# Cross and masked attention: the first scores issued right behind the first values, the squares turned back one step later

## The chip, the cores and the metric

The program runs on one core of a Trainium2 chip. The metric is the device time of one execution in microseconds (us); lower is better. A core has five engines that run their own instruction lists in order and meet at semaphores: TensorE (PE, with its weight loads shown apart as PEld), VectorE (DVE), ScalarE (ACT), GpSimd (POOL) and SyncE (SP), which issues the transfers.

## What is computed

The reference is a chain of four layers, each a cross attention and a feed-forward block, on x of 32 sequences x 128 tokens x 128 features, with a context of 32 x 128 x 96. The change touches the attentions of the first and of the third layer:

```python
x = x + _L0_xattn_ref(_layernorm(x), ctx_768, wq, bq, wk, bk, wv, bv, wo, bo)      # "cross"
...
x = x + _L2_xattn_ref(_layernorm(x), ctx_768, mask_BxS_bk0, Wq, Wkv)                # "masked"

def _L0_xattn_ref(x, y, wq, bq, wk, bk, wv, bv, wo, bo):     # 16 heads of 8 features
    q = x @ wq.T + bq;  k = y @ wk.T + bk;  v = y @ wv.T + bv
    ...
    score = jnp.einsum('bhqd,bhkd->bhqk', q, k) * scale
    attn = jax.nn.softmax(score, axis=-1)
    out = jnp.einsum('bhqk,bhkd->bhqd', attn, v)
    return out @ wo.T + bo
```

The masked one is the same without biases and without the output projection; rows that the mask leaves out get equal weights. Behind the first layer's attention stands a mixture of 8 experts, whose routing (a second layer norm, logits, the choice and the scatter of rows) rides along in the attention's loop.

## The kernel before, in words

The program is a row of phases. Each engine runs all of phase 1, then all of phase 2, and so on. `attention16` (line 310 on) builds three of them: "cross" (starts near 17 us and ends near 300 us of the profiled span), "masked" (near 787 to 1059 us) and "self". Only the first two use the branch that the change touches. "cross" carries the routing of the next block with it (`post` in the code), "masked" carries none.

The work is one sequence (an item, 128 x 128) at a time, 32 items, as a software pipeline written out by hand. `unrolled` yields one step after the other; in step t, `item(lag)` is item t - lag. So one step works on several items, each at another stage, and the order of the calls inside a step is the order in which an engine issues them. For these two phases F = 1, L = 2 and O = L + 4 = 6. One item passes through these stages:

- lag 0 and 1: `stats`, `aggregate` (DVE), `rsqrt` (POOL), `norm` (DVE, L288) give the layer norm h; `pe_hT` (PE, L404) turns h; `a_hT` (ACT, L941) copies it out; `pe_qkv` (PE, L415 and L416) multiplies with the weights of queries, keys and values; `v_qkv` (DVE: L602 and L615 in cross, L605, L607 and L618 in masked) evicts them.
- lag 2 (L): `pe_turn` (L424) turns q and k; `v_kx` (DVE, L708) expands the keys into kx, four masked copies; `a_qT` (ACT, L917) copies the turned queries, after kx. `pe_scores` (PE, L463) computes scores in two halves of 8 heads into the same two PSUM banks, only so that `v_max` (DVE, L716) can take each row's largest. The second half waits until the first maximum is read. `high` (DVE, L704) and `g_low` (POOL, L826) split q and k into exact parts.
- lag 3 (L + 1): `pe_stack_k` and `pe_stack_q` (PE, L430, eight matmuls) turn these parts. `pe_stack_q` waits for the second maximum. `a_qS` (ACT, L931, four copies) and `a_kS` (ACT, L923) copy them out.
- lag 4: `pe_scoresT` (PE, L478) computes the scores with keys on the partitions, in two halves, and `a_exp` (ACT, L954) takes the exponential of each.
- lag 5 (L + 3): `pe_values` (PE, L494) multiplies the first pair and the second pair of head columns with the values. `v_heads` (DVE, L724 and L726) turns the result in 32 x 32 squares and takes the reciprocal of the sums. `normed` (POOL, L736) divides. `v_heads_back` (DVE, L744) turns the squares back into oT.
- lag 6 (O): `pe_out` (PE, L519 in cross, L521 in masked) multiplies oT with the output weights, or only turns it; `v_residual` (DVE, L750) adds it to X.

In cross, `pe_post_route` (L2126, L2134 to L2140) and `pe_post_turn` (L2119) put the routing's matmuls into PE's step, and `v_post_rows` (L2216, L2235, L2223, and in some steps three or four small ones) and `v_route` put its vector work into DVE's.

Each engine's step is one straight list, for PE:

```python
for item in unrolled(last):
    if it := item(L):
        pe_turn(e, it)
    if it := item(L + 1):
        pe_stack_k(e, it)
        pe_stack_q(e, it)
    ...
    if it := item(F):
        pe_qkv(e, it)
    if it := item(O):
        pe_out(e, it)
    if it := item(L):
        pe_scores(e, it, 1)
```

For ACT the step is a_qT, a_qS, a_hT, (routing), a_kS, a_exp half 0, a_exp half 1, and for POOL rsqrt, the output bias (cross), g_low, normed, (routing).

Of the kernel before, what the change touches and what calls it, by code (L numbers as in the profile page):

```python
# [72 lines left out]
def build(nc, a, out):  # L73
    ctx = ExitStack()
    with ctx:
# [233 lines left out]
        def attention16(p, before, kind, post=None):  # L309
# [214 lines left out]
            def tensor(e):  # L524
                before(e)
                e.wait_ge(s_pad, at(s_pad, n_pad))
                e.wait_ge(sem(p + "weights"), 16 * n_loads[p[:2]])
                e.wait_ge(consts_ready, N_CONSTS)
                if post:
                    e.wait_ge(bf_ready, N_BF)  # L530
                if causal:
                    for item in unrolled(last):
                        if it := item(L + 2):
                            pe_scoresT(e, it, 0)
                        if it := item(L):
                            pe_turn(e, it)
                        if post:
                            pe_post_route(e, item)
                        if it := item(L + 3):
                            pe_values(e, it, 0)  # L540
# [4 lines that stand above are left out]
                            pe_scores(e, it, 0)  # L545
                        if it := item(L + 3):
                            pe_values(e, it, 1)
                        if post:
                            pe_post_turn(e, item)
                        if it := item(F):  # L550
                            pe_hT(e, it)
                        if it := item(L):
                            pe_scores(e, it, 1)
                        if it := item(G):
                            pe_gate(e, it)
                        if it := item(L + 2):
                            pe_scoresT(e, it, 1)
# [4 lines that stand above are left out]
                else:  # L562
# [6 lines that stand above are left out]
                        if post:  # L569
                            pe_post_route(e, item)  # L570
                        if it := item(L + 3):
                            pe_values(e, it, 0)
                        if post:
                            pe_post_turn(e, item)
                        if it := item(F):
                            pe_hT(e, it)
                        if it := item(L + 2):
                            pe_scoresT(e, it, 0)
                        if it := item(L):
                            pe_scores(e, it, 0)  # L580
                        if it := item(L + 3):
                            pe_values(e, it, 1)
                        if it := item(F):
# [5 lines that stand above are left out]
                        if it := item(L + 2):  # L589
                            pe_scoresT(e, it, 1)  # L590
# [166 lines left out]
            def vector(e):  # L757
# [5 lines left out]
                if causal:  # L763
                    e.tensor_scalar(w[p + "wo"][:, :], w[p + "wo"][:, :], 0.5, None, ALU.mult).then_inc(s_wo, 1)
                    for item in unrolled(last):
                        if it := item(0):
                            stats(e, it)
                        if it := item(F):
                            v_h2(e, it)
                        if post:  # L770
                            v_post_rows(e, item)
                        if it := item(L):
                            v_max(e, it, 0)
                        if it := item(1):
                            v_y(e, it)
                        if it := item(0):
                            aggregate(e, it)
                        if it := item(F + 1):
                            v_qk_norm(e, it)
                        if it := item(L + 3):  # L780
                            v_heads(e, it)
                            v_heads_back(e, it)
                        if post:
                            post["v_route"](e, item, O)
                        if it := item(L):
                            v_max(e, it, 1)
                        if it := item(F):
                            v_rotate(e, it)
                        if it := item(O):
                            v_residual_self(e, it)  # L790
                        if it := item(G):
                            v_gate(e, it)
                else:
                    for item in unrolled(last):
                        if it := item(L):
                            v_kx(e, it)
                        if it := item(0):
                            stats(e, it)
                        if it := item(F + 1):
                            high(e, it)  # L800
                        if it := item(1):
                            norm(e, it, h[:, it.s, :])
                        if post:
                            v_post_rows(e, item)
                        if it := item(L):
                            v_max(e, it, 0)
                        if it := item(0):
                            aggregate(e, it)
                        if it := item(L + 3):
                            v_heads(e, it)  # L810
                        if post:
                            post["v_route"](e, item, O)
                        if it := item(F):
                            v_qkv(e, it)
                        if it := item(O):
                            v_residual(e, it)
                        if it := item(L):
                            v_max(e, it, 1)
                        if it := item(L + 3):
                            v_heads_back(e, it)  # L820


            def g_low(e, it):
# [1962 lines left out]
```

## Time and profile before

| what | value |
|---|---|
| median of 3 runs | 1929.82 us (1918.54 to 1933.78) |
| the profiled execution, its own time | 1932.14 us |
| its span, first to last instruction | 1930.3 us |
| PE busy | 1573.1 us, 81% |
| DVE busy | 1325.4 us, 69% |
| ACT busy | 958.3 us, 50% |
| POOL busy | 858.7 us, 44% |
| mean granted TensorE clock | 0.879 of full speed |

Busy shares are means over phases with different limits. The granted clock is how much of TensorE's full clock of 2.4 GHz the chip gave; 0.50 is its lower level, 1.2 GHz. A matmul's duration is modelled at its end, so a PE that is shown busy is not PE at its peak. "Idle before" in a row is how long the engine had been idle when the instruction started, with what ended the wait; where it says "issue", the profile shows nothing that the engine waited for.

### The profile page before, as it was taken

To read this page: it belongs to the slowest core of one execution; us is meant where nothing else is said; L and a number is where in the kernel's file an instruction comes from. 1 tells how busy PE (TensorE), PEld (TensorE's weight loads), DVE (VectorE), ACT (ScalarE), POOL (GpSimd) and SP (SyncE) were. 2 spreads that over 40 slices of the span, in tenths; PEclk is the share of its full clock that TensorE was granted. 3 is DMA by queue.
4 is the path that set the end of the run, shared out by engine and by line. 5 is a ranking of instruction groups with operands and counts; after the bars stand their busy time and mean duration, and the time that the engine had idled before them with its cause. 6 is when DMAs were issued, how large, how long until landed. Compare 5 with 4: busy or idle time off the path is not lost. (4 is left out here: it accounts for less than half of the span.)

```text
span 1930.3 us, 37548 instructions
## 1 busy us (share of the span) xinstructions
PE 1573.1 (81%) x11614; PEld 1204.3 (62%) x11614; DVE 1325.4 (69%) x4215; ACT 958.3 (50%) x1953; POOL 858.7 (44%) x1432
## 2 busy tenths in 40 slices
PE   5889985977798989798897788888849699999840
PEld 3556664965677778565554455555539598888730
DVE  4886773348787777567764688888647488888522
ACT  2775562533333334357764577777725344444310
POOL 2444544356300000123322778788654555566426
PEclk9995786978899999669976699999969899999965
DMA  6674203821000000000000000000028100000043
GB/s 195 225 245 168 102 11 133 252 69 41 17 1 2 0 1 1 5 7 8 9 5 1 1 1 1 2 8 8 8 83 263 41 15 13 19 20 19 10 147 87
DMA packets 60786, 108.35 MB, mean 56 GB/s; under 512 B 11715, under 2 KB 49620, under 8 KB 59796
## 3 DMA queue, kind: packets, MB, share of 16 engines
q1 hardware_dynamic: 54452, 93.45, 15.3%
q0 software_dynamic: 6144, 12.60, 2.1%
q8 instruction: 92, 1.51, 0.3%
q14 instruction: 98, 0.80, 0.1%
HBM read 89.49 MB, written 52.17 MB: 73 GB/s over the span
## 5 line engine op out<-in xcount | busy, mean ns | idle before, releaser
L716 DVE TENSOR_REDUCE parts<-PS 128x8 fp32r<-128x1024 f32 x192 | 234.5, 1221 | 135.2 <-PE PS L463 134.8
L954 ACT ACTIVATE P<-PS 128x1024 f32<-128x1024 f32 x192 | 198.3, 1033 | 114.1 <-PE PS L478 114.1
L931 ACT CAST qS<-PS 32x512 fp32r<-32x512 f32 x384 | 220.7, 575 | 17.7 <-PE PS L430 14.3
L279 POOL TENSOR_TENSOR ve<-mv,eps_t 128x1 f32<-128x1 f32 x160 | 31.7, 198 | 349.7 <-DVE mv L275 349.4
L1788 DVE SCALAR_TENSOR_TENSOR X<-PS,wt,X 128x128 f32 (+1 forms) x480 | 134.4, 344 | 49.6 <-PE PS L1631 40.9
L478 PE MATMUL PS<-qS,kS 128*128 128x512 f32 x384 | 163.5, 484 | 0.8 <-ACT P L954 0.7
L1920 ACT ACTIVATE P<-PS,w_f_b 128x512 f32<-128x512 f32 x128 | 88.0, 687 | 142.7 <-PE PS L1612 141.2
L430 PE MATMUL PS<-ident_r,parts 128*128 128x128 f32 x768 | 134.1, 317 | 26.5 <-issue 12.9
L1631 PEld LDWEIGHTS PS<-w_f_w,P 128*128 128x128 f32 x1024 | 130.3, 193 | 39.8 <-issue 27.8
L1631 PE MATMUL PS<-w_f_w,P 128*128 128x128 f32 x1024 | 142.2, 283 | 13.7 <-DVE X L1788 11.8
L430 PEld LDWEIGHTS PS<-ident_r,parts 128*128 128x128 f32 x768 | 116.8, 226 | 47.9 <-POOL parts L826 26.1
L494 PE MATMUL PS<-P,vx 128*32 128x128 f32 x3072 | 142.1, 311 | 5.1 <-ACT P L954 5.0
L845 POOL TENSOR_TENSOR rrs<-rsq,neg_half 128x20 f32<-128x20 f32 x32 | 114.9, 3592 | 48.0 <-DVE rsq L646 47.4
L463 PE MATMUL PS<-kx,qT 32*128 32x512 f32 x384 | 110.4, 571 | 0.0
L494 PEld LDWEIGHTS PS<-P,vx 128*32 128x32 f32 x3072 | 82.5, 121 | 40.5 <-issue 28.3
L281 POOL TENSOR_TENSOR rstd<-ve,neg_half 128x1 f32<-128x1 f32 x160 | 89.9, 562 | 12.5
L826 POOL TENSOR_TENSOR parts<-qk,parts 128x128 fp32r<-128x128 f32 x192 | 84.6, 460 | 7.3 <-DVE parts L704 6.0
L478 PEld LDWEIGHTS PS<-qS,kS 128*128 128x128 f32 x384 | 72.5, 219 | 23.7 <-ACT P L954 11.7
L463 PEld LDWEIGHTS PS<-kx,qT 32*128 32x128 f32 x384 | 40.3, 207 | 71.5 <-issue 61.0
L1444 POOL TENSOR_TENSOR parts<-ident,mx 128x1024 fp32r<-128x1024 f32 x32 | 60.8, 1899 | 53.2 <-DVE mx L1383 53.2
L1843 POOL TENSOR_TENSOR ve<-mv,eps_t 128x4 f32<-128x4 f32 x8 | 1.6, 199 | 180.5 <-DVE mv L1699 180.5
L1319 PE MATMUL PS<-P 128*128 128x128 f32 x512 | 70.1, 280 | 6.5 <-DVE lgD L2263 2.9
(302 smaller groups left out, 4371.6 us busy)
## 6 DMA issues: line engine op xcount, KB each, us to landing
P<-in_f_blob SPq DMA_DIRECT2D x12, 578.0 KB, 4.1
Y<-in_f_blob SPq DMA_DIRECT2D x11, 578.0 KB, 4.4
ctxT<-in_ctxT SPq DMA_DIRECT2D x128, 48.0 KB, 1.7
tok<-hs SPq DMA_DIRECT2D x46, 128.0 KB, 3.4
hs<-yo SPq DMA_DIRECT2D x46, 128.0 KB, 4.1
P<-in_f_blob SPq DMA_DIRECT2D x12, 450.0 KB, 4.6
Y<-in_f_blob SPq DMA_DIRECT2D x11, 450.0 KB, 4.6
w_f_w<-in_f_w SPq DMA_DIRECT2D x2, 1024.0 KB, 5.7
```

The source lines that it names most:

```text
L281: q.tensor_tensor(rstd[:, it.s, :], ve[:, it.s, :], neg_half[:, 0:1], ALU.pow).then_inc(s_rs, 1)
L430: m = e.matmul(TP[which][:, g * T:(g + 1) * T], parts[:, it.s, which, 4 * g:4 * g + 4, :, :].rearrange("p h c d -> p (h c d)"), ident_r[:, ...
L463: m = e.matmul(S_ps[:, i, :], qT[r:r + 32, it.s, :], kx[r:r + 32, it.s % 2, :, :].rearrange("p j t -> p (j t)"), start=not causal, stop=True)
L478: m = e.matmul(ST_ps[:, i, :], kS[:, it.s % 2, g, :], qS[:, it.s % 2, g, :, :].rearrange("p j t -> p (j t)"), start=not causal, stop=True)
L494: m = e.matmul(OB[32 * g:32 * g + 32, pair * T:(pair + 1) * T], vx[:, it.s, 128 * j + 32 * g:128 * j + 32 * g + 32], P[:, it.s % 2, 4 * g ...
L716: e.tensor_reduce(parts[:, it.s, 0, 8 * half:8 * half + 8, 3, 0], S_ps[:, :, :].rearrange("p i (j t) -> p (i j) t", t=T), AXX, ALU.max)\
L845: e.tensor_tensor(rrs[:, :], rsq[:, :], neg_half[:, 0:n_heads], ALU.pow).then_inc(s_rs3, 1)
L931: m = e.copy(qS[r, it.s % 2, :, j, :], TP[0][r, :].rearrange("p (g t) -> p g t", g=4))
L954: e.activation(P[:, it.s % 2, 8 * half:8 * half + 8, :].rearrange("p h t -> p (h t)"), ST_ps[:, :, :].rearrange("p j n -> p (j n)"), ACT.E ...
L1631: m = e.matmul(YP[(n_steps * b + x) % 2][:, s * T:(s + 1) * T], lhs, w2[:, x, t * D:(t + 1) * D], start=(t == 0), stop=(t == tiles - 1))
L1788: m = e.scalar_tensor_tensor(out=X_s, in0=rows, scalar=wt[:, b, s, x:x + 1], in1=X_s, op0=ALU.mult, op1=ALU.add)
L1920: e.activation(gt[:, (x % 2) * tiles + t, :], ZP[i % 4][:, :], ACT.Gelu if kind == "gelu" else ACT.Relu, bias=b1[:, x, t:t + 1]).then_inc( ...
```

## The change

Two calls move, each within its engine's step, in the branch of cross and masked attention. No instruction is added, removed or altered.

```diff
@@ tensor(e), the step of PE
                         if it := item(L + 3):
                             pe_values(e, it, 0)
+                        if it := item(L):
+                            pe_scores(e, it, 0)
                         if post:
                             pe_post_turn(e, item)
                         if it := item(F):
                             pe_hT(e, it)
                         if it := item(L + 2):
                             pe_scoresT(e, it, 0)
-                        if it := item(L):
-                            pe_scores(e, it, 0)
                         if it := item(L + 3):
                             pe_values(e, it, 1)
@@ vector(e), the step of DVE
                         if it := item(F + 1):
                             high(e, it)
+                        if it := item(O):
+                            v_heads_back(e, it)
                         if it := item(1):
                             norm(e, it, h[:, it.s, :])
...
                         if it := item(L):
                             v_max(e, it, 1)
-                        if it := item(L + 3):
-                            v_heads_back(e, it)
```

On PE, in the cross phase behind the stacks of one step, the rows were (L494 the values, L2119 the routing's turn, L404 the turn of h, L478 the scores with keys on the partitions, L463 the scores for the maximum):

```order
L494 MATMUL PS<-P,vx 32x128 [waits values_turned,v,exp]
L494 MATMUL PS<-P,vx 32x128 x7
L2119 MATMUL PS<-ident,hD 128x128 [waits hT,qT,d_h,kx,v]
L404 MATMUL PS<-ident,h 128x128 [waits qT,kx,h]
L478 MATMUL PS<-qS,kS 128x512 [waits exp,qS,kS]
L478 MATMUL PS<-qS,kS 128x512
L463 MATMUL PS<-kx,qT 128x512 [waits mx,kx,qT]
L463 MATMUL PS<-kx,qT 128x512
L494 MATMUL PS<-P,vx 32x128 x8
```

and now are:

```order
L494 MATMUL PS<-P,vx 32x128 [waits values_turned,v,exp]
L494 MATMUL PS<-P,vx 32x128 x7
L463 MATMUL PS<-kx,qT 128x512 [waits mx,kx,qT]
L463 MATMUL PS<-kx,qT 128x512
L2119 MATMUL PS<-ident,hD 128x128 [waits hT,qT,d_h,kx,v]
L404 MATMUL PS<-ident,h 128x128 [waits qT,kx,h]
L478 MATMUL PS<-qS,kS 128x512 [waits exp,qS,kS]
L478 MATMUL PS<-qS,kS 128x512
L494 MATMUL PS<-P,vx 32x128 x8
```

The two L463 rows moved ahead of four others, with the same waits. In masked the L2119 row is absent and the rest is the same.

On DVE, in the cross phase from one step's second maximum to the next step's first, the rows were (L744 turns the squares back, L708 expands the keys, L288 writes h):

```order
L716 TENSOR_REDUCE parts<-PS 128x8 [waits s]
L744 STREAM_TRANSPOSE oT<-oN 128x128 [waits values_normed,out]
L708 TENSOR_TENSOR kx<-PS,jmask 128x512 [waits turn]
L268 BN_STATS bn<-X 128x6 [waits h]
L704 CAST parts<-qk 128x32x24 [waits qkf,tq]
L288 TENSOR_SCALAR h<-X,mv,rstd 128x128 [waits rstd,bn,hps]
L2216 BN_STATS bnD<-X 128x6 [waits done]
L2235 TENSOR_SCALAR hD<-X,mvD,rsD 128x128 [waits d_rstd]
L2223 BN_AGGR mvD<-bnD 128x2 [waits d_bn]
L716 TENSOR_REDUCE parts<-PS 128x8 [waits s,tq]
```

and now are:

```order
L716 TENSOR_REDUCE parts<-PS 128x8 [waits s]
L708 TENSOR_TENSOR kx<-PS,jmask 128x512 [waits turn]
L268 BN_STATS bn<-X 128x6 [waits h]
L704 CAST parts<-qk 128x32x24 [waits qkf,tq]
L744 STREAM_TRANSPOSE oT<-oN 128x128 [waits values_normed,out]
L288 TENSOR_SCALAR h<-X,mv,rstd 128x128 [waits rstd,bn,hps]
L2216 BN_STATS bnD<-X 128x6 [waits done]
L2235 TENSOR_SCALAR hD<-X,mvD,rsD 128x128 [waits d_rstd]
L2223 BN_AGGR mvD<-bnD 128x2 [waits d_bn]
L716 TENSOR_REDUCE parts<-PS 128x8 [waits s,tq]
```

L744 moved behind L708, L268 and L704; between the second maximum and the keys' expansion nothing is left. The lists of ACT, POOL and SP are as before.

## Rows read from the trace of the kernel before

**Rows 1.** The page: granted TensorE clock in 40 slices of 48.3 us.
```profile
PEclk9995786978899999669976699999969899999965
```

**Rows 2.** DVE's L708 by stretch: us, DVE busy (x instructions), PEclk, DMA share, GB/s.
```profile
43.05:145.52 102.47, 9.18 (x14) 1.00 0.71 240
145.52:195.65 50.13, 3.42 (x5) 0.56 0.45 155
195.65:210.50 14.85, 1.30 (x2) 1.00 0.62 222
210.50:250.26 39.76, 2.73 (x4) 0.57 0.12 41
250.26:271.99 21.73, 1.96 (x4) 1.00 0.03 11
...
859.77:985.38 125.61, 11.74 (x19) 1.00 0.03 8
985.38:1031.78 46.40, 3.46 (x5) 0.56 0.01 2
```

**Rows 3.** All engines, masked: us, PE, PEld, DVE, ACT, POOL busy, PEclk, DMA.
```profile
813.53:852.12 38.59, 38.59 (x225) 24.93 (x225) 23.01 (x56) 21.04 (x37) 8.34 (x24) 0.50 0.02 6
859.77:985.38 125.61, 110.71 (x1009) 66.49 (x1010) 99.78 (x254) 93.07 (x162) 37.54 (x108) 1.00 0.03 8
```

**Rows 4.** Waits of DVE, masked, 859.77 to 985.38 us: us in total, times, longest.
```profile
DVE parts L716 <- PE PS L463: 25.2, 18, 1.4
```

**Rows 5.** Waits of DVE, cross, 43.05 to 145.52 us.
```profile
DVE parts L716 <- PE PS L463: 11.7, 14, 2.0
DVE oT L744 <- POOL oN L736: 3.8, 14, 0.5
```

**Rows 6.** Timeline of one masked step: start, us, instructions, [idle before <-releaser].
```profile
922.33 0.30 DVE L744 STREAM_TRANSPOSE oT<-oN 128x128 f32<-128x128 f32 x1
...
922.52 0.63 PE L430 MATMUL PS<-ident_r,parts 128*128 128x128 f32 x4 [0.21 <-issue]
922.56 0.65 DVE L708 TENSOR_TENSOR kx<-PS,jmask 128x512 fp32r<-128x512 f32 x1
...
923.08 0.64 PE L494 MATMUL PS<-P,vx 128*32 128x128 f32 x16
...
923.24 0.27 ACT L917 CAST qT<-PS 128x128 fp32r<-128x128 f32 x1 [0.86 <-DVE kx L708]
...
923.41 2.34 ACT L931 CAST qS<-PS 32x512 fp32r<-32x512 f32 x4
923.78 0.34 DVE L288 TENSOR_SCALAR h<-X,mv,rstd 128x128 f32<-128x128 f32 x1
...
924.91 0.50 PE L463 MATMUL PS<-kx,qT 32*128 32x512 f32 x2
...
925.53 1.23 DVE L716 TENSOR_REDUCE parts<-PS 128x8 fp32r<-128x1024 f32 x1 [1.40 <-PE PS L463]
...
926.41 0.60 PE L416 MATMUL PS<-w_a_wkv,ctxT 96*128 96x256 f32 x2
...
927.38 0.29 DVE L605 TENSOR_SCALAR qk<-PS,keep 128x128 f32<-128x128 f32 x1
```

**Rows 7.** Timeline of one cross step, same columns; PE's first.
```profile
108.15 1.11 PE L430 MATMUL PS<-ident_r,parts 128*128 128x128 f32 x8 [0.32 <-POOL parts L826]
...
112.96 0.60 PE L416 MATMUL PS<-w_a_wkv,ctxT 96*128 96x256 f32 x2
```

**Rows 8.** The same cross step on DVE.
```profile
108.70 0.31 DVE L744 STREAM_TRANSPOSE oT<-oN 128x128 f32<-128x128 f32 x1 [0.26 <-POOL oN L736]
108.94 0.65 DVE L708 TENSOR_TENSOR kx<-PS,jmask 128x512 fp32r<-128x512 f32 x1
...
113.80 0.41 DVE L602 TENSOR_TENSOR qk<-PS,w_a_bqk 128x256 f32<-128x256 f32 x1
```

**Rows 9.** The same cross step on ACT.
```profile
109.79 2.34 ACT L931 CAST qS<-PS 32x512 fp32r<-32x512 f32 x4
```

## The prediction

> **What bounds the two phases.** I read the granted clock over the span first, then stretches of the two phases, then the waits of DVE, then one step of each in order of time. The clock matters because the two phases are where it moves [rows 1]: of the slices of 48.3 us, the fourth to the sixth (cross) show 5, 7 and 8 tenths, the 17th and 18th and the 21st and 22nd (masked) 6, 6, 7 and 6, while the long phases behind (24 to 29, 31 on) stay at 9 and 8. Counted by the keys' expansion L708, one per step, the phases fall into stretches at either level [rows 2]: cross runs 14 + 2 + 3 = 19 steps at the full 2.4 GHz (the stretch to 271.99 counts the step that begins at its edge), at 102.47 / 14 = 7.32 us each in the long one, and 5 + 4 steps mostly at 1.2 GHz, 50.13 / 5 = 10.03 and 39.76 / 4 = 9.94 us each. Masked runs 18 at the full clock (19 with the edge), 125.61 / 18 = 6.98 us each, and 5 at 46.40 / 5 = 9.28; further ones at 1.2 GHz stand at its start.
>
> At 1.2 GHz, PE is the bound: it is shown busy for 38.59 of 38.59 us [rows 3]. At 2.4 GHz it is busy for 110.71 of 125.61 us, 88%, and something else sets the step. In masked DVE has one wait in its step, 25.2 / 18 = 1.40 us before the first maximum L716 [rows 4]; all else that it does is back to back. In cross it has two, 11.7 / 14 = 0.84 before the same L716 and 3.8 / 14 = 0.27 before L744, which waits for POOL's quotients: 1.11 together [rows 5]. So the loop at full clock is DVE's work, plus the detour over PE to the first scores. One masked step shows the detour [rows 6]: L288 writes h until 924.12, PE then turns h and does one half of the other scores, L463 runs from 924.91 to 925.41, and L716 starts at 925.53, 0.12 behind. Yet L463 needs nothing of h. Its inputs are kx (done 923.21) and qT (done 923.51), and PE's first values end at 923.72.
>
> **The change part by part, masked.** L463 moves behind those values: it can run from 923.72 to 924.22, and L716 starts at 924.34 instead of 925.53, 1.19 earlier. DVE gets there in time: L744 takes a slot of 922.56 - 922.33 = 0.23 us, and moving it from ahead of L708 to ahead of L288 leaves L288's end at 924.12. Behind L463, PE's turn of h slips from 924.18 to about 924.2: nothing, since ACT copies h out only behind its four copies L931 (923.41 to 925.75).
>
> How much of 1.19 survives is set by what is late next. DVE's eviction L605 (927.38) needs the products L416, which end at 927.01. With the latency of 0.12 seen above it could start at 927.13, so 0.25 is free. L416 in turn hangs on ACT: its end is 3.60 behind L931's start, over the four copies, the copy of h and PE's products. L931 follows qT and the second stack L430. qT moves by L744's slot, 0.23, which is the second part of the change. The stack ends at 923.15 and doesn't move, because it waits for the second maximum. So L931 starts at about 923.15 + 0.12 = 923.27 instead of 923.41, 0.14 earlier. Together 0.25 + 0.14 = 0.39 us a step, and a step of 6.59. The new loop is: second maximum, stack of q, four copies, copy of h, products, eviction, second maximum. Of DVE's 1.40 of waiting about 1.0 stays, most of it before L605 now.
>
> 18 steps x 0.39 = 7.0 us.
>
> **Cross.** Here L744 costs more than its slot of 108.94 - 108.70 = 0.24: it waited 0.26 for POOL first [rows 8]. One step later POOL's quotients are long there, so L708 comes 0.50 earlier and takes qT along. L931 started at 109.79 [rows 9]; now the stack is its bound, which ends at 109.26 [rows 7]: 109.38, so 0.41 earlier. L416 ends at 113.56 [rows 7] and the eviction L602 started at 113.80: 0.24 - 0.12 = 0.12 free. That is 0.53. The stack here waited for POOL's parts L826, which follow the first maximum through DVE's and POOL's statistics and so move by more than the rest. That can give up to another 0.1; I take 0.55, a step of 6.77. The routing's turn L2119 now stands behind L463 too, and its reader on ACT is behind the same four copies: nothing.
>
> 19 steps x 0.55 = 10.5 us.
>
> **The rest.** In steps at 1.2 GHz PE is full and its work is unchanged: 0. In some six of the 14 in [rows 2] the clock changes on the way; at 0.25 each, about half of the gain above, they give 1.5. Fill and drain are left at 0: L744 is late by a step, but the output product that reads it was always in that later step. No row shows L463 directly behind the values; that may cost PE an idle gap as the 0.21 before L430 in [rows 6], 37 x 0.21 = 7.8 us if it all fell on the loop, or, since no work is added, nothing. I take nothing, because PE has slack in the step, and keep 7.8 for the range. From below, the gain is bounded by DVE's waits themselves, priced as a rival.
>
> Sum: 7.0 + 10.5 + 1.5 = 19.0. Against the profiled execution's own 1932.1 us (span 1930.3) that is 1913.1. That execution is 2.3 above the median of the runs, so I forecast 1911 us.
>
> **Rivals.** All are shifted by the same 2.3.
>
> (a) The full clock lasts longer. The clock fell in cross and in masked at 88% busy and came back after 40 to 50 us with PE full. With steps of 6.77 and 6.59, PE is denser at full clock. If the stretches at 1.2 GHz of [rows 2] went away, the 9 cross steps would take 9 x 6.77 = 60.9 instead of 89.9 us and the 5 masked ones 33.0 instead of 46.4: 42.4 us less, 1870. One stretch fewer gives 1895 to 1898. For it: it fell at the smaller load of 88% and came back only with PE full. Against it: it stays up in slices 24 to 29 [rows 1] too, in the self attention, whose step has waits like these, so it isn't a matter of the waits alone.
> The Trainium skill, "TensorE: Matmul & The Clock Gate", Part 1: The HAM clock gate, says that the lower level is the default and that activity of TensorE is what lifts it; by that rule denser steps go toward this rival. The trace agrees in that the clock came back only out of stretches with PE full.
>
> (b) ACT's chain gives way too, and all of DVE's waiting goes: 19 x 1.11 + 18 x 1.40 = 46.3 us, 1884. Against it: the chain from L931 to L416, 3.60 us, is untouched.
>
> (c) L931 doesn't move, because the stack is later than I think, and only the free 0.25 and 0.12 are won: 18 x 0.25 + 19 x 0.12 = 6.8 us, 1923.
>
> (d) Slower: the clock falls more often. The changed steps reach a fall of the clock in another state, and each phase gets one more stretch of five steps at 1.2 GHz: 5 x (10.03 - 6.77) + 5 x (9.28 - 6.59) = 29.8 us against 19.0 won, 1940. Slower than before begins with the seventh further step at the lower level (19.0 / 3.1), and by over 1% with the thirteenth. For it: three of the four full-clock stretches in [rows 2] ended at a fall in the midst of like steps. Against it: the rule above, and that PE gets denser.
>
> **How the numbers follow.** The forecast gets 0.43, (a) 0.27, (b) 0.06, (c) 0.12, (d) 0.12. A measurement of this kernel tells about 1%, 19 us, from no change. The forecast lies just there (18.8 below the median); its own range, with the clock's stretches moving by some steps, is 1900 to 1922, about half of it faster by over 1%. So faster: 0.27 + 0.06 + 0.22 = 0.55. Slower by over 1%: a third of (d), 0.04, and 0.01 for the unforeseen: 0.05. The rest, 0.40, is within 1%. The range holds most of (a) and half of (d): 1873 to 1930.
>
> **What would show it.** In the changed profile: masked steps of about 6.6 us at full clock and cross steps of about 6.8; L463 right behind the first values on PE; L716's first wait down from 1.40 and 0.84 to 0.3 or less; no wait before L744; a new wait of DVE before L605 and L602 for L416; L931 released by L430 rather than by qT; steps at 1.2 GHz unchanged, with stretches at 9.3 to 10.0 us a step. Wrong would be: steps near 5.6 to 6.2 us without a wait on L416 (then b), L931 still released by qT, or a sum of full-clock steps that differs from 37 by more than five (then a or d decides the total, whatever the step gives).

## The result and the profile after

The changed kernel takes 1865.79 us (median of 4 runs, 1863.75 to 1870.34). The kernel before took 1928.89 in its runs beside it (1918.54 to 1933.78). The ratio is 0.968, with a 95% interval of 0.964 to 0.973. The forecast was 1911, and its range began at 1873: the gain is over three times as large as forecast. The profiled execution is the one of 1870.34 us; its span is 1868.5, 61.8 shorter than before's 1930.3. Every version has one profile only, while the time of one kernel varies from execution to execution: before's medians in the rounds below lie between 1911 and 1929 us, so each ratio is taken against before's own runs of its round.

The page of after first, with the granted clock over the span. A slice is 46.7 us now.

```profile
PEclk9999969978899999699985999999879899999965
```

The slices of the cross phase, the second to the fifth, and of the masked one, the eighteenth to the twenty-first, show 9 and 8 tenths, where [rows 1] shows three and four slices between 5 and 8. What is left near the two phases are the sixth slice, 234 to 280 us, behind cross, the seventeenth, 747 to 794 us, in the fill of masked, and the twenty-second, 981 to 1028 us, behind masked. Next the stretches counted by the keys' expansion L708 (stretch, its length, DVE's busy time on L708 with its count, granted clock, DMA share, GB/s), each from the fifth L708 of its phase to the last. The kernel before, cross and masked:

```profile
50.91:271.99 221.08, 17.89 (x28) 0.82 0.47 158
823.02:1031.78 208.76, 17.96 (x27) 0.83 0.02 7
```

And after:

```profile
51.32:231.76 180.44, 18.41 (x27) 1.00 0.57 190
785.49:965.07 179.58, 18.45 (x27) 1.00 0.03 8
```

All of these are 27 steps (a stretch that begins and ends at an L708 counts 27 or 28 instructions). The clock of 1.00 is the main finding: behind the fill of each phase no step runs at 1.2 GHz any more. So 40.6 us went in cross and 29.2 in masked, 69.8 together. They can be split at before's own pace at full clock [rows 2]: 27 steps of 94.61 / 13 = 7.28 us (the long cross stretch from 50.91 us on, without its first step of 7.86) are 196.6, and 27 of 6.98 are 188.5. From there down to 180.44 and 179.58 the steps themselves are shorter: 16.1 + 8.9 = 25.0 us. From 221.08 and 208.76 down to there it is the clock: 24.5 + 20.3 = 44.8 us, nearly two thirds of the gain. In masked this has two parts. Before's first four steps of the stretch, 823.02 to 859.77, took 36.75 us instead of 4 x 6.98 = 27.9, because the clock came up only at 854 us, deep in the phase; in after it was up before the fifth L708. That is 8.8 us, and the late fall [rows 2] is the other 11.5. Some 8 of the 69.8 come back outside these stretches: between the phases it is 553.7 us instead of 551.0, behind masked 903.4 instead of 898.5. Over all versions below these two vary by more (547.8 to 556.2, and 897.8 to 904.4), so no cause is looked for.

The masked step after, by time (start, duration, engine, line, operation, idle time ahead with its releaser). It answers to [rows 6]:

```profile
852.00 0.69 DVE L708 TENSOR_TENSOR kx<-PS,jmask 128x512 fp32r<-128x512 f32 x1
852.19 0.63 PE L430 MATMUL PS<-ident_r,parts 128*128 128x128 f32 x4 [0.47 <-issue]
...
852.92 2.34 ACT L931 CAST qS<-PS 32x512 fp32r<-32x512 f32 x4
853.25 0.31 DVE L744 STREAM_TRANSPOSE oT<-oN 128x128 f32<-128x128 f32 x1
853.33 0.50 PE L463 MATMUL PS<-kx,qT 32*128 32x512 f32 x2
...
853.94 1.23 DVE L716 TENSOR_REDUCE parts<-PS 128x8 fp32r<-128x1024 f32 x1
...
855.28 0.27 ACT L941 COPY hT<-PS 128x128 f32<-128x128 f32 x1
855.60 0.49 PE L415 MATMUL PS<-w_a_wq,hT 128*128 128x128 f32 x2 [0.37 <-ACT hT L941]
...
855.93 0.60 PE L416 MATMUL PS<-w_a_wkv,ctxT 96*128 96x256 f32 x2
856.11 0.87 POOL L826 TENSOR_TENSOR parts<-qk,parts 128x128 fp32r<-128x128 f32 x2
...
856.66 0.35 DVE L605 TENSOR_SCALAR qk<-PS,keep 128x128 f32<-128x128 f32 x1 [0.63 <-POOL parts L826]
...
857.52 1.22 DVE L716 TENSOR_REDUCE parts<-PS 128x8 fp32r<-128x1024 f32 x1
```

L463 ends at 853.83 and the first L716 starts at 853.94, 0.11 behind it and with no idle time noted. L931 starts 0.10 after the stack L430 ends at 852.82 (qT would have released it hardly sooner: L931 stands 0.20 behind L917's start at 852.72, and stood 0.17 behind it before); from L931 to the end of L416 (856.53) it is 3.61, to be compared with 3.60 before. DVE's wait has moved to L605. DVE's waits of some 25 steps of each phase, all that the view lists (masked 795 to 960 us, cross 57.84 to 231.76):

```profile
DVE qk L605 <- POOL parts L826: 15.8, 25, 0.6
...
DVE qk L602 <- PE PS L416: 5.8, 13, 0.7
```

The first line is of masked: 0.63 a step, where [rows 4] had 1.40 before L716. The second is of cross, where 13 of the 26 steps have the wait; L716 and L744 of [rows 5] have none left. The name in the first line is a trap. L826 ends its work well behind L605's start (856.98 against 856.66), so only one of its two halves could release it; L416 ended 0.13 ahead of L605, about the gap that L716 has behind L463 (0.11). A version below that brings L416 forward shortens this wait to 0.2, and then the view names L416.

### The profile page after: what moved, and what is told of

It is laid out like the page before. It is cut to its first block and busy times, and to the rows that moved or that the text cites. A ratio compares the mean times of both kernels' runs of the same rounds, so it can differ in the third digit from the quotient of the medians.

```text
span 1868.5 us, 37548 instructions
## 1 busy us (share of the span) xinstructions
PE 1506.6 (81%) x11614; PEld 1169.2 (63%) x11614; DVE 1329.3 (71%) x4215; ACT 959.9 (51%) x1953; POOL 860.5 (46%) x1432
## 3 DMA queue, kind: packets, MB, share of 16 engines
q1 hardware_dynamic: 54452, 93.45, 16.1%
## 5 line engine op out<-in xcount | busy, mean ns | idle before, releaser
L716 DVE TENSOR_REDUCE parts<-PS 128x8 fp32r<-128x1024 f32 x192 | 234.1, 1219 | 42.4 <-PE PS L463 38.0
L931 ACT CAST qS<-PS 32x512 fp32r<-32x512 f32 x384 | 221.2, 576 | 6.8 <-PE PS L430 3.5
L1631 PEld LDWEIGHTS PS<-w_f_w,P 128*128 128x128 f32 x1024 | 130.4, 193 | 39.8 <-issue 27.9
L478 PE MATMUL PS<-qS,kS 128*128 128x512 f32 x384 | 149.3, 444 | 1.0 <-ACT P L954 1.0
L430 PE MATMUL PS<-ident_r,parts 128*128 128x128 f32 x768 | 124.3, 293 | 30.7 <-issue 25.2
L430 PEld LDWEIGHTS PS<-ident_r,parts 128*128 128x128 f32 x768 | 105.0, 201 | 48.2 <-issue 36.3
L494 PE MATMUL PS<-P,vx 128*32 128x128 f32 x3072 | 129.9, 290 | 4.4 <-ACT P L954 4.4
L494 PEld LDWEIGHTS PS<-P,vx 128*32 128x32 f32 x3072 | 76.1, 113 | 42.9 <-issue 32.5
L463 PE MATMUL PS<-kx,qT 32*128 32x512 f32 x384 | 101.2, 523 | 2.2 <-ACT qT L917 2.2
L826 POOL TENSOR_TENSOR parts<-qk,parts 128x128 fp32r<-128x128 f32 x192 | 84.7, 461 | 7.7 <-DVE parts L704 6.4
L478 PEld LDWEIGHTS PS<-qS,kS 128*128 128x128 f32 x384 | 65.9, 199 | 21.3 <-ACT P L954 16.1
L2542 POOL DMA_INDIRECT G<-hs,idx x64 | 63.7, 995 | 22.7 <-issue 13.5
```

Of the source, the lines that this page charges most:

```text
L430: m = e.matmul(TP[which][:, g * T:(g + 1) * T], parts[:, it.s, which, 4 * g:4 * g + 4, :, :].rearrange("p h c d -> p (h c d)"), ident_r[:, ...
L463: m = e.matmul(S_ps[:, i, :], qT[r:r + 32, it.s, :], kx[r:r + 32, it.s % 2, :, :].rearrange("p j t -> p (j t)"), start=not causal, stop=True)
L478: m = e.matmul(ST_ps[:, i, :], kS[:, it.s % 2, g, :], qS[:, it.s % 2, g, :, :].rearrange("p j t -> p (j t)"), start=not causal, stop=True)
L494: m = e.matmul(OB[32 * g:32 * g + 32, pair * T:(pair + 1) * T], vx[:, it.s, 128 * j + 32 * g:128 * j + 32 * g + 32], P[:, it.s % 2, 4 * g ...
L716: e.tensor_reduce(parts[:, it.s, 0, 8 * half:8 * half + 8, 3, 0], S_ps[:, :, :].rearrange("p i (j t) -> p (i j) t", t=T), AXX, ALU.max)\
L931: m = e.copy(qS[r, it.s % 2, :, j, :], TP[0][r, :].rearrange("p (g t) -> p g t", g=4))
```

## The experiments

**One part of the change alone.** `e1_scores_only` leaves the squares where they were:

```diff
-                        if it := item(O):
-                            v_heads_back(e, it)
...
                             v_max(e, it, 1)
+                        if it := item(L + 3):
+                            v_heads_back(e, it)
```

> The kernel before with only the first scores moved up on PE; L744 stays ahead of the keys' expansion. Theory A (the clock stays full because the same PE work is done in shorter steps; the step itself is set by the chain over ACT's four copies L931): masked steps at full clock go from 6.98 to about 6.73 us, since only the 0.25 us of slack before L605 is won, cross steps from 7.32 to 6.8 to 7.1. The clock stays up in at least one of the phases, total 1870 to 1900 us. Rival B (the order on DVE, not the step length, matters to the clock): the clock falls as before, total 1915 to 1925.

`e2_squares_only` leaves the scores where they were:

```diff
                             pe_values(e, it, 0)
-                        if it := item(L):
-                            pe_scores(e, it, 0)
...
                             pe_scoresT(e, it, 0)
+                        if it := item(L):
+                            pe_scores(e, it, 0)
```

> The kernel before with only L744 moved behind the keys' expansion on DVE. Theory A: masked steps stay at 6.98 us, as the detour over h to the first scores is untouched; cross loses the 0.27 us of waiting for POOL, 7.05. Clock stretches at 1.2 GHz stay as before, total 1918 to 1930 us. Rival B (the squares' place is what matters): masked steps under 6.9 us and no stretch at 1.2 GHz, total under 1890.

e1: 1886.51 us, ratio 0.981 (0.976 to 0.986). e2: 1903.55, ratio 0.989 (0.981 to 0.997). The stretches of L708 in e1, cross and masked, 26 steps each, from the sixth L708 on:

```profile
61.06:240.13 179.07, 16.93 (x27) 1.00 0.52 177
801.91:978.85 176.94, 16.89 (x27) 1.00 0.03 8
```

That is 6.89 and 6.81 us a step at full clock throughout; the clock and the total are as expected, the masked step is 0.08 longer. In e2 cross is first, then masked in three stretches:

```profile
67.84:241.52 173.68, 16.96 (x25) 1.00 0.54 183
829.01:891.75 62.74, 6.11 (x10) 1.00 0.03 8
891.75:938.15 46.40, 3.44 (x6) 0.56 0.02 6
938.15:1000.80 62.65, 6.11 (x9) 1.00 0.02 5
```

Cross runs at 173.68 / 25 = 6.95 with no fall. In masked the squares alone leave the step as it was, 62.74 / 9 = 6.97, and the clock falls for five steps (46.40 us). The expectation missed e2's total for want of cross's clock; its steps were right to 0.1. So with either part alone cross kept the clock, and only with the scores did masked.

**Each phase by itself.** `e6_masked_only` has the new orders in masked and the old ones in cross:

```diff
-                        if it := item(L):
+                        if masked and (it := item(L)):
                             pe_scores(e, it, 0)
...
+                        if has_bias and (it := item(L)):
+                            pe_scores(e, it, 0)
...
-                        if it := item(O):
+                        if masked and (it := item(O)):
                             v_heads_back(e, it)
...
+                        if has_bias and (it := item(L + 3)):
+                            v_heads_back(e, it)
```

> The new orders of PE and DVE in the masked phase alone; cross has the orders of the kernel before. If the clock of each phase depends on that phase's own steps, masked has 6.65 us steps and no stretch at 1.2 GHz behind its fill, cross has its 7.3 and 10 us steps as before, and the total is 1866 + about 40 = 1895 to 1915 us. If the phases share something (what cross does before decides whether masked falls), masked shows stretches at 1.2 GHz and the total is over 1915.

Measured: 1908.26 us over 10 runs (1890.27 to 1940.21), ratio 0.992 (0.988 to 0.997). Two stretches of cross and the one of masked:

```profile
68.64:223.16 154.52, 13.70 (x22) 1.00 0.60 203
223.16:262.54 39.38, 2.73 (x5) 0.57 0.02 8
817.81:990.65 172.84, 17.66 (x26) 1.00 0.03 8
```

Masked is that of after: 26 steps of 6.65, no fall. Cross has before's steps, 154.52 / 21 = 7.36, and falls late, once. So the gain of the clock is made in each phase separately. This profile is of the fastest of the ten runs, 18 us below the median; the others show a lower mean clock (0.87 to 0.90 against 0.91). That its cross ran 21 such steps before it fell, and that eight of the ten runs spread from 1890 to 1918 us, shows that before's pace is one at which falls come and go. It also shows the uncertainty of the split above: at 7.36 us, a pace from more steps, 2 of the 45 us would count as steps and not as clock.

**Is it the length of the step?** Theory A: the clock stays up because steps are shorter, so PE is loaded more densely. Theory C: it stays up because of the new order on PE, whatever the length. `e3_after_slowed` keeps the new order and gives DVE idle work:

```diff
                         if it := item(L):
+                            for i in range(3 if has_bias else 2):
+                                e.transpose(sg[:, 0, i * T:(i + 1) * T], ident[:, :])
                             v_max(e, it, 1)
```

> The changed kernel with idle work put on DVE ahead of the second maximum (three 32x32-square turns of a constant per step in cross, two in masked, about 0.23 us each), so that its steps are as long as before: 7.3 to 7.4 us in cross, about 7.1 in masked, with PE's new order kept. Theory A (step length, so PE's work per time, decides the clock): stretches at 1.2 GHz come back, total 1920 to 1940 us. Rival C (PE's new order, with its waits in other places, keeps the clock up whatever the step length): the clock stays at 1.00 behind the fill, total 1866 + 32 x 0.65 + 32 x 0.46 = about 1902 us.

`e9_one_delay` has one such operation in both phases, `e10_long_delay` five:

```diff
-                            for i in range(3 if has_bias else 2):
-                                e.transpose(sg[:, 0, i * T:(i + 1) * T], ident[:, :])
+                            for i in range(5):
+                                e.transpose(sg[:, i // 4, (i % 4) * T:(i % 4 + 1) * T], ident[:, :])
```

> The changed kernel with one piece of idle work on DVE per step: steps of about 6.85 us in both phases. Theory (falls of the clock begin between steps of 6.94, where no trace so far has one, and 6.97): no fall behind the fill, total 1866 + 32 x 0.15 + 32 x 0.18 = 1877 us. Rival (any lengthening brings falls in proportion): some falls, over 1885 us.

> The changed kernel with five pieces of idle work on DVE per step: steps of about 7.75 us in both phases, PE's order and work unchanged. Theory A (less PE work per time, more falls): falls of the clock more often or longer than in the slowed version with 7.28 and 7.04 us, total well over the 1934 us that steps of 7.75 alone would give (1866 + 64 x 1.07), 1945 to 1970. Rival (a rhythm: falls come where the step stands in a bad relation to something fixed on the chip, and not at other lengths): no falls, 1934 us.

e9: 1874.86 us, ratio 0.972 (0.967 to 0.978). e3: 1903.87, 0.988 (0.985 to 0.992). e10: 2014.14, 1.047 (1.040 to 1.054). Their stretches, cross and masked, of e9 (26 steps each, 6.88 and 6.85 us):

```profile
58.09:236.89 178.80, 17.51 (x27) 1.00 0.53 178
795.54:973.57 178.03, 17.49 (x27) 1.00 0.03 8
```

of e3 (26 each; steps without a fall are 7.28 and 7.04):

```profile
58.90:253.43 194.53, 17.49 (x26) 0.96 0.48 164
808.22:997.93 189.71, 17.49 (x27) 0.94 0.03 7
```

and of e10 (24 and 26 steps; those without a fall are 7.66 and 7.62, the means 9.0 and 9.35):

```profile
79.33:295.44 216.11, 16.14 (x25) 0.79 0.42 142
857.63:1100.80 243.17, 17.50 (x27) 0.67 0.02 6
```

The order is the same in all three; only DVE's idle work differs. At 6.9 us no fall; at 7.0 to 7.3 falls of a single step, every fifth in cross and every second or fifth in masked; at 7.6 falls in much of the phase. Within the new order that is theory A, and e10 is its strongest case. The longer steps by themselves would cost about 1 us in each of 32 + 32 steps, 62 us, and the version is 148 above after: some 86 are the clock. But e3 fits neither theory fully. At before's step lengths its falls are short, while those of before last four or five steps, and its clock is up at the fifth masked step as in after, where before's was not. In all the falls cost e3 about 12 us between the fifth and the last L708 of the two phases (201.6 us against 27 steps of 7.1 to 7.3 in cross, 196.8 against 27 of 7.04 in masked), where before lost 45. So giving the steps their old length back brought only about a quarter of the clock's loss back, and its total, 1904, is the one that theory C gave. The length of the step decides whether the clock falls in the new order; something in the order itself, which no run isolates, sets how much a fall costs.

**Is it PE's load?** `e4_before_filled` leaves before's orders and adds three matmuls of no use, which write an unused part of PSUM, ahead of PE's wait for h:

```diff
                             pe_values(e, it, 0)
+                            for i in range(3):
+                                e.matmul(OB[:, 2 * T:3 * T], ident_r[:, :], ident_r[:, :], start=True, stop=True)
```

> The kernel before with three more 128x128x128 matmuls of a constant per step on PE, behind the first values, where PE waits 0.46 us for h at full clock; nothing reads them. Steps at full clock stay at 7.3 and 6.98 us. Theory A in its form 'more PE work per time keeps the clock': no or fewer stretches at 1.2 GHz, total 1885 to 1905 us. If only shorter steps help, or the clock answers to something else than PE's load, the stretches stay and each of their steps is about 0.4 us longer: 1930 to 1940 us.

1897.49 us (1889.45 to 1917.53), ratio 0.987 (0.976 to 0.998), as expected. One stretch each, and L463 of one step ahead of the first stretch and one in it:

```profile
93.49:262.99 169.50, 14.99 (x23) 1.00 0.48 162
816.43:1004.45 188.02, 17.60 (x27) 1.00 0.03 8
...
78.80 0.79 PE L463 MATMUL PS<-kx,qT 32*128 32x512 f32 x2
...
98.26 0.50 PE L463 MATMUL PS<-kx,qT 32*128 32x512 f32 x2
```

The masked steps are before's, 188.02 / 27 = 6.96, and none falls. In cross none of the 23 steps from 93.49 us on falls either, at 169.50 / 23 = 7.37 us each, where before fell twice. But cross came to full clock late: up to 87 us L463 takes 0.79 us instead of 0.50, and before was there at 45 us. (PEclk reads 1.00 in these first steps of every version, because the trace has no record of the clock ahead of its first rise; there the durations tell the level.) The kernel before gets faster by being given work. `e7_slowed_filled` does the same to e3, behind the first scores:

```diff
                             pe_scores(e, it, 0)
+                        if item(L + 3):
+                            for i in range(3):
+                                e.matmul(OB[:, 2 * T:3 * T], ident_r[:, :], ident_r[:, :], start=True, stop=True)
```

> The slowed version of the changed kernel (the idle work on DVE) with the three further matmuls of a constant on PE behind the first scores. The slowed version had steps of 7.28 and 7.04 us and fell to 1.2 GHz for one step in every five or so. Theory A (more PE work per time keeps the clock): the falls go, or become rare, with the same 7.28 and 7.04 us steps, total about 1904 - 12 = 1892 us. Rival (the rhythm of the steps, not the load, makes the falls): falls as often as before, total 1904 us or more, since matmuls added at 1.2 GHz cost time.

1947.46 us, ratio 1.011 (1.003 to 1.018): a clear miss. The stretches of e7, 24 steps each:

```profile
78.90:261.37 182.47, 16.15 (x25) 0.95 0.50 168
813.95:1028.07 214.12, 16.36 (x24) 0.68 0.02 7
```

The steps at full clock are e3's; the clock falls at least as often, and the masked steps at the low level take 10.3 to 10.5 us, each with the filler's work at half speed in it. At the start of masked PE was full and the clock stayed low all the same:

```profile
813.95:868.20 54.25, 54.25 (x319) 36.73 (x318) 32.98 (x86) 28.53 (x49) 10.64 (x30) 0.50 0.02 6
```

This is what the expectation's rival, a rhythm of the steps, had said. The falls do come at even intervals: every fifth step, 37.5 us apart, in e3's cross, and every fourth, 30.7 us, in e7's. A rhythm by itself isn't shown either, since e9, e3 and e10 go from no falls to many with the length. PE's longest wait, ahead of L430, was untouched by the filler, 0.9 us in e3 and in e7 (e3's masked from 830.4 to 858.5 us, four steps, then e7's from 1014.0 to 1049.2, five, all at full clock):

```profile
PE PS L430 <- issue: 3.5, 4, 0.9
PE PS L415 <- ACT hT L943: 1.5, 4, 0.4
...
PE PS L430 <- issue: 4.3, 5, 0.9
```

What the filler took was the wait ahead of L415, which is gone from e7's list. `e12_long_filled` therefore puts filler into e10 where the trace shows PE waiting, for the second maximum ahead of the stack of q, in masked alone:

```diff
                             pe_stack_k(e, it)
+                            if masked and (old := item(L + 3)):
+                                if due(old.n):
+                                    e.wait_ge(s_tv, at(s_tv, old.n))
+                                for i in range(6):
+                                    e.matmul(OB[:, 2 * T:3 * T], ident_r[:, :], ident_r[:, :], start=True, stop=True)
                             pe_stack_q(e, it)
```

> The long-delay version (steps of 7.66 and 7.62 us) with six more 128x128x128 matmuls of a constant per masked step, put where PE waits over 1 us for the second maximum, between the stacks; nothing reads them. Theory 'PE's load keeps the clock': masked runs at 2.4 GHz throughout, 28 steps take about 214 instead of 254 us, total about 1975 us. Theory 'only the length of the step counts, or filling with such matmuls is no load to the clock': masked falls as often as before, about 254 us or more, total about 2014 us.

1994.95 us, ratio 1.041 (1.033 to 1.049). The wait ahead of L430 is down from 1.3 us in e10 to 0.8. Of e12 the masked stretch, 25 steps:

```profile
893.56:1091.70 198.14, 16.83 (x25) 0.94 0.02 7
```

198.14 / 25 = 7.93 us a step at a clock of 0.94, against 9.35 at 0.67 in e10. From the first to the last of 32 steps it is 251.6 us against 283.8. So with load in PE's wait the clock stays up most of the time at steps of 7.6, with seven falls of a single step, where e10's masked was low for two thirds of the time; the expectation had no fall at all. This rests on one profile each. The totals can't bear it, since the intervals of the two ratios overlap (1.040 to 1.054, and 1.033 to 1.049), and cross, whose code is e10's, took 298.4 us from its first to its last L708 in e12 and 275.0 in e10. Why e7's filler prevented no fall is open; that it left PE's longest wait as it was is a difference from e12 that the traces show, no more.

**What bounds the new step?** After this change the prediction's loop over L931 was the candidate. `e5_turn_copy_early` puts ACT's copy of h between the third and fourth copy of L931:

```diff
                         if it := item(L + 1):
-                            a_qS(e, it)
+                            a_qS_begin(e, it)
                         if it := item(F):
...
                         if it := item(L + 1):
+                            a_qS_copies(e, it, (3,))
                             a_kS(e, it)
```

> The changed kernel with one more move, on ACT: the copy of h's turn (and in cross the routing's) goes between the third and the fourth of the four copies L931 instead of behind them. Theory (the step is now set by the chain second maximum, stack, four copies, copy of h, products, eviction; one copy of 0.58 us leaves it): masked steps go from 6.65 to about 6.1 us, where the chain over the copy of the keys and the first exponential is next, cross steps from 6.69 to about 6.35, where DVE is nearly full; DVE's wait before L605 and L602 goes. Total 1866 - 32 x 0.55 - 32 x 0.34 = about 1838 us. Rival (L605 waits for POOL's parts L826, as the trace names, or another chain is as long): masked steps stay above 6.5 us, total over 1858.

`e8_last_copy_late` also moves the fourth copy behind the first exponentials, and `e11_after_two_copies` puts the copy of h behind two of the four (its edit is shown against e8):

```diff
                             a_exp(e, it, 0)
+                        if it := item(L + 1):
+                            a_qS_copies(e, it, (3,))
```

> The version with the early copy of h's turn, and with the fourth copy of L931 moved again, between the two exponentials, where ACT waits 0.9 us for scores. Theory (in that version the step is set by the chain stack, copies, copy of the keys, first exponential, second half of the scores, turn, stack; this move takes 0.58 us out of it): masked steps go from 6.21 to 5.8 us, where DVE is full, cross steps from about 6.6 to about 6.4, and the clock stays up; total about 1857 - 27 x 0.4 - 27 x 0.15 = 1842 us. Rival (DVE is already the bound in that version): no change, 1857 us.

```diff
-                a_qS_copies(e, it, range(3))
+                a_qS_copies(e, it, range(2))
...
                         if it := item(L + 1):
+                            a_qS_copies(e, it, (2,))
                             a_kS(e, it)
```

> As the version with the last copy late, but the copy of h's turn already behind the second of the four copies L931; it may then wait some 0.1 us for PE's turn of h. Theory (in both versions before, masked is still set by second maximum, stack of q, copies up to h's, products, eviction: 0.73 + 1.72 + 0.17 + 0.3 + 0.92 + 0.14 + 0.85 + 1.22 is 6.05 of the 6.21 us): masked steps go to about 5.85 us, where DVE is full; cross, full on DVE already, changes by less than 0.1. Total 1847 - 27 x 0.35 = about 1838 us. Rival (DVE's own work is the 6.21): no change, 1847 us.

e5: 1857.18 us, ratio 0.964 (0.959 to 0.970). e8: 1847.12, 0.957 (0.952 to 0.962). e11: 1841.32, 0.962 (0.957 to 0.967). All three beat before. Against the changed kernel (0.964 to 0.973) only e8's interval lies clear; those of e5 and e11 overlap with it. e8 and e11 ran beside different runs of before, and their intervals overlap, so neither is shown better. The masked step is 6.20 to 6.21 in all of them (e5: 155.09 / 25), 0.44 below after. For e5 6.1 was expected in masked, and 6.35 in cross, where it is 164.55 / 25 = 6.58; its total came out 19 us above what was expected, and its profile is of the fastest of its seven runs, 9.5 us below the median. For e8 and e11 a step of 5.8 to 5.85 was expected, and nothing moved. DVE's waits of e5, 795 to 960 us:

```profile
DVE parts L716 <- PE PS L463: 6.4, 26, 0.7
DVE qk L605 <- PE PS L416: 4.7, 25, 0.2
```

Now L605 waits 0.2 and for L416. The masked step of e11 shows why a still earlier copy gains nothing (its L951 is the copy of h):

```profile
850.26 0.30 DVE L288 TENSOR_SCALAR h<-X,mv,rstd 128x128 f32<-128x128 f32 x1
850.62 0.33 PE L404 MATMUL PS<-ident,h 128*128 128x128 f32 x1
850.72 0.70 PE L478 MATMUL PS<-qS,kS 128*128 128x512 f32 x2
851.04 0.27 ACT L951 COPY hT<-PS 128x128 f32<-128x128 f32 x1 [0.19 <-PE PS L404]
851.35 0.64 PE L494 MATMUL PS<-P,vx 128*32 128x128 f32 x16
851.93 0.49 PE L415 MATMUL PS<-w_a_wq,hT 128*128 128x128 f32 x2
852.25 0.60 PE L416 MATMUL PS<-w_a_wkv,ctxT 96*128 96x256 f32 x2
852.99 0.35 DVE L605 TENSOR_SCALAR qk<-PS,keep 128x128 f32<-128x128 f32 x1 [0.19 <-PE PS L416]
```

The copy of h is done at 851.31, but L415 starts at 851.93: behind the turn L404, PE's queue has L478 and the second values L494 first. By this trace the bound is PE's order from DVE's h on, no longer ACT; no run changes that order to test it. From L708's start to L415's start it is 3.60 in after and 3.16 to 3.17 in e8 and e11; the difference, 0.44, is that of the steps.

## Why the prediction was wrong

The step that failed is the one on the clock: "In steps at 1.2 GHz PE is full and its work is unchanged: 0", with the stretches of [rows 2] carried over as they stood. A step that is wholly at 1.2 GHz did stay as long (the fourth masked step is 9.49 us in before, e2, e5 and e8); what changed is how many there are, from nine in each phase behind the fill, some of them in part, to none. The sum thus priced shorter steps at a fixed clock, while the clock depends on the step: 44.8 of the 69.8 us are there. Rival (a) named the mechanism and got 0.27. Its argument against itself (self attention keeps the clock with waits like these) was weak, since it spoke of other steps; its argument for itself, that the clock fell where PE had gaps, is borne out by e9, e3 and e10, where the same work of PE stands in longer steps, and by e4 and e12, and not by e7. That it comes back once PE is full is not enough: in e7 it stayed low through 54 us of full PE. The Trainium skill, "TensorE: Matmul & The Clock Gate", Part 1: The HAM clock gate, lets activity of TensorE lift the clock; the order of lengths and falls in e9, e3 and e10 agrees with it, and e7, with its 54.25 us of full PE at a clock of 0.50, doesn't fit.

Rival (a) was also priced too small, at 1870. It counted nine cross steps and five masked ones. The masked phase has four further ones at its start, of 38.59 / 4 = 9.65 us each [rows 3]: 4 x (9.65 - 6.65) = 12 us, so 1858. (Some 9 of the 12 came; the first of the four is part of the fill and took 9.08 in after.) Measured were 1866, and the range's floor of 1873 cut off even the 1870.

Point by point for the steps:

- **Masked, 0.39 a step, 6.59 expected: 6.65 measured.** The detour over PE is gone, L463 stands behind the first values with no gap, the stack and no longer qT releases L931 (by 0.03), and the wait is before L605, all as stated. The 0.06 that is missing lies behind L605: from it to the second maximum 0.86 instead of 0.80.
- **Cross, 0.55 a step, 6.77 expected: 6.68.** The wait before L744 is gone, the wait before L602 for L416 is there in half of the steps (5.8 / 13 = 0.45). The stack moved a little too, the "another 0.1" that was left out: it ends 1.95 and 1.96 us behind the start of the second maximum in two steps of after (from 123.30 and 129.99), and 2.03 before (from 107.23).
- **The number of steps.** 25.0 us come from steps against 19.0 forecast: the terms were about right, but since no step stays at 1.2 GHz, they count on 54 and not on 37. Cross brings 16.1 against 10.5, masked 8.9 against 7.0.
- **Order on PE, 0 with 7.8 kept open:** 0 holds; PE isn't idle ahead of L463, and L716 follows it directly.
- **Rival (b)** did not come: the chain from L931 is 3.61, unchanged, and e5 shows that it was the bound of the new masked step. **(c)** did not come, since L931 moved. **(d)**, a clock that falls more often, has its mechanism in e3 and e10, but on the other side: it needs longer steps, and this change made them shorter.
- **A reading that was off:** the prediction has the clock at 9 and 8 tenths from slice 31 on [rows 1]; slices 39 and 40 show 6 and 5. No term hangs on it.

Open are three things: why the falls of e3 last one step and those of before and e2 four or five; why filler helped in e4 and e12 and not in e7; and when the clock comes up in a phase's start. In masked it was up by the fifth L708 in after and at steps of 7.04 in e3 alike, but only by the ninth in before and e2 and the eleventh in e7, so the step's length doesn't order that, and the 8.8 us of it are not explained by any run here. The profile's busy time of PE doesn't order the cases. Masked in after has no fall at this load, all engines in order PE, PEld, DVE, ACT, POOL:

```profile
792.14:965.07 172.93, 150.35 (x1456) 97.06 (x1456) 150.63 (x363) 135.47 (x235) 53.51 (x154) 1.00 0.03 8
```

That is 150.35 / 172.93 = 87% for PE, less than the 88% at which before fell [rows 3].

## What to carry to other kernels

Where stretches of like steps run at two granted clocks, the clock is a result of the step and no constant: price a shorter step both at a fixed clock and with all half-clock steps gone, count every one of those (the fill's too), and let the range hold both. The sign goes the other way as well: a delay in a loop whose PE waits can cost more than itself, as e10's 1 us a step cost more than 2. Look for the next bound in the in-order queue of the engine that is waited for: here a ready copy of h stood behind products that nobody was waiting for yet.

## What the runs showed of the hardware

- In steps of up to 6.95 us on the mean the granted clock never fell behind the fill in any profiled run (after, e1, e2's cross, e5, e6's masked, e8, e9, e11; e5's other six runs are 6 to 10 us slower than the profiled one, at mean clocks of 0.903 to 0.910 against 0.912, so it isn't shown for them); at 6.96 to 6.98 it fell in two phases of three (before's and e2's masked, not e4's); from 7.04 on it fell somewhere in every phase but e4's filled cross (23 steps of 7.37 without a fall); at 7.6 it fell through much of both in e10 (0.79 and 0.67 on the mean). The same steps can hold for long: e6's cross ran 21 of 7.36 before it fell.
- PE's busy share as the profile shows it doesn't say which: 87% without a fall (after, masked), 88% with (before).
- With matmuls of no use where PE waits, before's masked phase kept the clock (e4), and e10's went from 0.67 to 0.94 (e12), one profile each; ahead of a shorter wait, with the longest one left (e7), they lengthened the half-clock steps to 10.4 us and prevented no fall. In e4's masked phase the steps at full clock are no longer for them, 6.96 against 6.98.
- A full PE doesn't bring the clock back soon in every case: in e7's masked phase it stayed at 0.50 over 54.25 us in which PE was busy without a gap; in before's over the 38.59 us of [rows 3].
- PEclk can read 1.00 where TensorE is at the low level: ahead of the first record of a trace. In e4 L463 takes 0.79 us up to 87 us, and 0.50 from then on.
